# Row statistics of the feed-forward one step later, and two banks of attention products copied in one VectorE operation

## The reference, cut to what matters

```python
x = x + recurrence(layernorm(x))                 # tanh recurrence, 512 time steps, 8 sequences of 512 x 128
y = layernorm(x)
for i in range(6):                               # depth
    y = attn_layer(shift_tokens(y), Wqkv[i], q_scale[i], k_scale[i], Wo[i]) + y
    y = ffn_layer(shift_tokens(y), ln_g[i], ln_b[i], W1[i], b1[i], W2[i], b2[i]) + y
x = x + y

def attn_layer(x, ...):                          # 16 heads of 64, windows of 32 tokens
    q, k, v = split(x @ Wqkv)
    q, k = l2norm(q) * qs, l2norm(k) * ksc       # then rotary tables with cos, sin and a scale
    out = local_attention(q, k, v)               # each window of 32 queries sees its own and the window before
    return out @ Wo
def ffn_layer(x, g, bln, W1, b1, W2, b2):        # 128 -> 2 x 341 -> 128
    xn = (x - mean(x)) / sqrt(var(x) + 1e-5) * g + bln
    a, gate = split(xn @ W1 + b1)
    return a * gelu(gate) @ W2 + b2
```

## Time and profile before

| | before |
|---|---|
| time, median of 3 runs | 3390.91 us (3388.34 to 3396.97) |
| profiled execution, its own time | 3384.15 us |
| its span, first to last instruction | 3382.4 us |
| granted TensorE clock, mean | 0.993 of full speed |
| PE busy | 3262.9 us, 96% of the span |
| DVE busy | 2728.5 us, 81% |
| POOL busy | 2563.7 us, 76% |
| ACT busy | 2227.8 us, 66% |

### The profile page before, as it was taken

How to read it: one execution, slowest core, us unless ns; L and a number is a source line. 1 busy time by engine, 2 the same in 40 slices (tenths; PEclk the granted TensorE clock), 3 DMA queues, 4 the chain that set the end, 5 groups by cost and what they waited for, 6 DMA issues and landing times. The chain is left out here.

```text
span 3382.4 us, 101399 instructions
## 1 busy us (share of the span) xinstructions
PE 3262.9 (96%) x42193; PEld 2153.0 (64%) x42193; DVE 2728.5 (81%) x3698; ACT 2227.8 (66%) x4397; POOL 2563.7 (76%) x2957
## 2 busy tenths in 40 slices
PE   8999699999999999999999999999999999999996
PEld 5555366666666666666666666666666666666664
DVE  2333598888988888888888888888888888888883
ACT  2222367767777777776776777777767777777674
POOL 0000498888888888888888888888888888888882
PEclk9999899999999999999999999999999999999999
DMA  3000001000001000001000010000010000000000
GB/s 74 1 1 1 4 11 36 12 11 8 12 17 36 8 11 11 11 15 36 11 12 8 11 42 12 10 9 11 11 43 8 12 11 11 12 13 18 14 9 13
DMA packets 62284, 52.53 MB, mean 16 GB/s; under 512 B 11526, under 2 KB 59396, under 8 KB 61828
## 3 DMA queue, kind: packets, MB, share of 16 engines
q1 hardware_dynamic: 61828, 46.05, 5.2%
HBM read 43.93 MB, written 2.10 MB: 14 GB/s over the span
## 5 line engine op out<-in xcount | busy, mean ns | idle before, releaser
L477 POOL TENSOR_TENSOR cosp<-cosp,sinp 128x1024 f32<-128x1024 f32 x384 | 905.6, 2373 | 26.5 <-DVE sinp L976 24.3
L584 PE MATMUL ps<-w_qk,xs 128*128 128x512 f32 x1536 | 747.8, 609 | 11.6 <-ACT sq L792 7.9
L688 PEld LDWEIGHTS ps<-px,w_vo 128*128 128x128 f32 x6144 | 701.0, 192 | 54.2 <-ACT px L833 38.8
L467 POOL TENSOR_TENSOR cosp<-cosp,rr 128x1024 f32<-128x1024 f32 x384 | 723.1, 1904 | 11.4
L688 PE MATMUL ps<-px,w_vo 128*128 128x128 f32 x6144 | 721.8, 276 | 3.7 <-ACT px L833 1.7
L973 DVE TENSOR_TENSOR cosp<-ps,tab 128x1024 f32<-128x1024 f32 x384 | 469.9, 1224 | 253.5 <-PE ps L584 250.2
L792 ACT ACTIVATE sq<-ps 128x1024 f32<-128x1024 f32 x384 | 393.4, 1024 | 338.1 <-DVE sinp L976 338.1
L584 PEld LDWEIGHTS ps<-w_qk,xs 128*128 128x128 f32 x1536 | 262.9, 191 | 342.9 <-issue 342.9
L976 DVE TENSOR_TENSOR sinp<-ps,tab 128x1024 f32<-128x1024 f32 x384 | 466.5, 1215 | 0.0
L737 PE MATMUL ps<-pT,xtm 32*128 32x512 f32 x3072 | 435.5, 615 | 24.4 <-DVE pT L1050 13.4
L982 DVE TENSOR_REDUCE ss<-sq 128x16 f32<-128x1024 f32 x384 | 454.5, 1184 | 3.1 <-POOL rr L452 1.8
(11 more groups left out here) (110 smaller groups left out, 4760.8 us busy)
## 6 DMA issues: line engine op xcount, KB each, us to landing
tab<-in_tab SPq DMA_DIRECT2D x96, 128.0 KB, 2.1
qks<-in_scales SPq DMA_DIRECT2D x96, 128.0 KB, 3.5
w_qk<-in_L_ffn_Wqkv SPq DMA_DIRECT2D x12, 512.0 KB, 6.4
w_v<-in_wv_t SPq DMA_DIRECT2D x6, 512.0 KB, 8.0
w_o<-in_L_ffn_Wo SPq DMA_DIRECT2D x6, 512.0 KB, 8.4
x<-in_L_attn_x SPq DMA_DIRECT2D x16, 128.0 KB, 6.0
out<-w_v SPq DMA_DIRECT2D x16, 128.0 KB, 2.5
w<-in_L_ffn_W SPq DMA_DIRECT2D x6, 341.0 KB
```

The costliest lines, as they stand in the source:

```text
L467: eng.tensor_tensor(v, v, rr[:, B % 2, HEADS * i:HEADS * i + HEADS].unsqueeze(2).to_broadcast([P, HEADS, DH]), ALU.mult).then_inc(rot_read ...
L477: eng.tensor_tensor(cosp[:, A % 2, i, :], cosp[:, A % 2, i, :], sinp[:, i, :], ALU.add).then_inc(rot_added, 1)
L584: t = eng.matmul(ps[:, u, :], xs[:, n % ROUND, :], w_qk[:, n // TILES % 2, i, 512 * u:512 * u + 512], start=True, stop=True)
L688: t = eng.matmul(Y, w_vo[:, E // TILES % 2, i // HP, i % HP, :], px[:, i, :], start=i == 0, stop=i == HEADS - 1)
```

## The change

It does two things. The statistics of a turn move from lag 7 to lag 8: on VectorE from behind the gated product to a place between the residual sum of E and the rotary multiplications of the keys; with them the four extra columns of the inverse root (ScalarE and GpSimd) move from step 4T+7 to 4T+8, `shift` to 4T+9, and ScalarE's normalisation to step 4T+9, between its copies to `qT` and its copies to `kT`. And ScalarE copies two banks of products instead of three, while VectorE copies banks 1 and 2 in one operation of 128x1024. TensorE's order stays the same; two of its waits count differently.

```diff
-        normed = lambda s: min(s, NT) * REFINE
-        rooted = lambda s: min(s, NT) * 2
+        rounds_before = lambda s: min(s, NT) + (s > NT) + (s > NT + ROUND)
+        normed = lambda s: rounds_before(s) * REFINE
+        rooted = lambda s: rounds_before(s) * 2
...
@@ GpSimd step
-                T = turn_of(s, 8)
+                T = turn_of(s, 9)
                 if T is not None:
-                    eng.wait_ge(norm_step, normed(s) if s <= NT else normed(s) + REFINE)
+                    eng.wait_ge(norm_step, normed(s))
                     after(eng, xn_ready, TB * T)
                     eng.wait_ge(variance_done, 2 * T + 2)
-                    eng.tensor_tensor(shift[:, :], nmean[:, :], rr[:, 1, 2 * HEADS:], ALU.mult).then_inc(shift_done, 1)
+                    eng.tensor_tensor(shift[:, :], nmean[:, :], rr[:, 0, 2 * HEADS:], ALU.mult).then_inc(shift_done, 1)
...
-                T = turn_of(s, 7)
+                T = turn_of(s, 8)
                 if T is not None:
                     eng.wait_ge(stat_step, 2 * TB * T + 2 * TB)
...
@@ TensorE step
-                    after(eng, px_evac, 3 * E + 2)
+                    after(eng, px_evac, 2 * E + 2)
                     eng.transpose(X, xs[:, C % ROUND, :], ident[:, :]).then_inc(xt_done, 1)
                 if tile(E):
-                    eng.wait_ge(px_evac, 3 * (E + 1))
+                    eng.wait_ge(px_evac, 2 * (E + 1))
                     eng.wait_ge(px_last, E + 1)
...
@@ ScalarE
+            def normalised(T):
+                eng.wait_ge(shift_done, T + 1)
+                eng.wait_ge(rows_evac, T + 1)
+                after(eng, cols_done, T)
+                for i in range(TB):
+                    at = 2 * HEADS + i
+                    eng.activation(xn[:, i, :], xr[:, i, :], ACT.Identity, bias=shift[:, i:i + 1], scale=rr[:, 0, at:at + 1]).then_inc(xn_ready, 1)
...
-                    for i, b in enumerate((3, 0, 1)):
+                    for i, b in enumerate((3, 0)):
                         eng.wait_ge(px_done, 4 * E + i + 1)
...
+                    if turn_of(s, 9) is not None:
+                        normalised(turn_of(s, 9))
                     if turn_of(s, 10) is not None:
                         eng.activation(warm[:, 1:2], warm[:, 0:1], ACT.Gelu)
                     for u, k in enumerate(K_BANKS):
...
@@ VectorE step
+                T8 = turn_of(s, 8)
+                if T8 is not None:
+                    statistics(T8)
                 if tile(A):
                     rope(A, 1)
...
-                T7, T13 = turn_of(s, 7), turn_of(s, 13)
-                if T7 is not None:
-                    statistics(T7)
+                T13 = turn_of(s, 13)
                 if T13 is not None:
                     update(T13)
...
-                    eng.tensor_copy(px[:, :, 64:96], G(2).rearrange("p (h q) -> p h q", q=WIN)).then_inc(px_last, 1)
+                    eng.tensor_copy(px[:, :, 32:96].rearrange("p h (b q) -> p b h q", q=WIN),
+                                    ps[:, 5:7, :].rearrange("p b (h q) -> p b h q", q=WIN)).then_inc(px_last, 1)
```

More of the change, by code:

```diff
@@ L794, in ffn @@
             def ffn(s):
[L795 to L802, removed]
                 T = turn_of(s, 9)
@@ L873, in step @@
                         eng.copy(dst, G(k).rearrange("p (h b t) -> p h b t", h=4, b=GB)).then_inc(turn_evac, 1)
+                T = turn_of(s, 9)
+                if T is not None and not tile(B):
+                    normalised(T)
                 T = turn_of(s, 7)
```

## The result

The changed kernel takes 3406.11 us (median of 6 runs, 3404.15 to 3411.69), the kernel before beside it 3389.28: ratio 1.005, 95% interval 1.0037 to 1.0062. It is slower by 0.5%, where "no change" was the forecast and 3392 the number; it lies 0.9 us inside the upper end of the range, 3407. The profiled execution took 3411.69 us, the longest of its six, with a span of 3409.9 us.

What follows compares the result with a forecast made beforehand. TensorE was taken as held in step mod 0 by GpSimd, late behind VectorE's statistics. Terms -29 (mod 0), +27 (mod 1), +8 (mod 2), -5 (results) sum to +1: 3385 profiled, 3392 as median, range 3372 to 3407.

Steps and rivals of the forecast that it cites:

- no change: Whole kernel: measured time within 0.3% (about 10 us) of the kernel before, chance 0.60.
- step mod 0: Steps with s mod 4 = 0: statistics no longer delay GpSimd's chain and the query turning; 16.07 becomes 15.23 us, gain 0.84.
- the query rotary starts at 2.47: VectorE, every step: behind the longer copy the query rotary starts at 2.47 us instead of 2.02, 0.45 later.
- the new wait for the normalisation: Steps mod 1: TensorE's `xn` transposes wait 0.58 us for ScalarE's normalisations, in 46 rounds: +27 us.
- VectorE did not become the bound: Rival, every step: no idle time left on VectorE, so the longer copy costs 102 us, 3493; chance 0.03.
- the steps with a result: Last five rounds: the result's sum no longer stands behind the statistics on VectorE; 1.05 us forward each, -5 us.
- 6.37 + 0.65 + 8.68 = 15.70: Steps mod 0 in the 20 rounds with fused weights: key projection, fusing, rest of step; 16.33 becomes 15.70, gain 0.63.
- The gelus: Steps mod 2: ScalarE's last two gelus end about 0.40 later, next step starts 0.24 later; 35 rounds, +8 us.
- The holes: TensorE inside the scores: 19 holes of about 0.9 us, about 11 in steps mod 2 covering the gelu delay.
- 46 rounds that have all parts: Basis of the sum: per-step gains and losses over 46 pipeline rounds, plus the last rounds, together +1 us.
- The same 0.45: ScalarE behind the query rotary: the squares of the queries and all behind move 0.45 us; squares hidden by 0.5.
- a dearer copy: Rival: VectorE's two-bank copy costs more than 1.22 us; at 1.37 it gives +21, 3413; chance 0.12.

Runs made afterwards that it cites:

- Run 3: Changed kernel with ScalarE's four normalisations moved right behind the exponential in step 4T+9: 3376.15 us, ratio 0.9963 to the kernel before.
- run 7: Changed kernel with 32 unused transposes (64 TensorE instructions) added at its start, shifting the instruction blocks: 3409.02 us, ratio 1.0061 to the kernel before.
- run 8: Kernel before with the same 32 unused transposes (64 TensorE instructions) added at its start: 3389.94 us, ratio 1.0009 to the kernel before.
- Run 2: Kernel before with only the copies changed (ScalarE two banks, VectorE two in one operation), statistics and normalisation unmoved: 3399.92 us, ratio 1.0031.
- run 5: Kernel of run 3 with ScalarE's copies `xc` also moved behind the exponential in steps mod 3: 3366.04 us, ratio 0.9933 to the kernel before.
- run 9: Kernel before with an extra ScalarE scratch copy of 0.42 us ahead of the copies to qT in steps mod 3: 3389.66 us, ratio 1.0003.
- run 10: Kernel before with the same extra ScalarE copy, but between the copies to qT and those to kT, in steps mod 3: 3394.13 us, ratio 1.0016.
- run 1: Changed kernel with the copies put back (ScalarE three banks, VectorE one), so only the statistics and normalisation move: 3367.60 us, ratio 0.9938 to the kernel before.
- run 4: Kernel of run 1 with ScalarE's normalisations moved behind the exponential in step 4T+9: 3359.43 us, ratio 0.9915 to the kernel before.

## Why the prediction was right and where it failed

**Right.** The step mod 0 was held by the statistics: the key projection is back at 6.37 and the step gains 0.86 (forecast 0.84). The copy costs 1.220, the query rotary starts at 2.47, the new wait for the normalisation is there in 46 rounds and costs 0.62 (0.58). Run 3, which takes that wait away, confirms its price. VectorE did not become the bound: the step mod 3 is still 14.40, and 0.80 of idle time is left in the step mod 1. In the last rounds the steps with a result went from 16.15 to 15.11, the 1.05 of the forecast. In the usual steps the sum is +1.8 for tiles 12 to 167, against a forecast of +1 for the pipeline.

**Mis-sized.** "6.37 + 0.65 + 8.68 = 15.70" for fused rounds: with the fusing in front, the output starts 0.74 later than in a round without it (2097.87 - 2095.20 = 2.67 against 2036.44 - 2034.51 = 1.93) and takes 0.1 longer, and the step is 15.90. That is 20 x 0.2 = 4 us. The gelus, "+0.24" a step, cost 0.07: in 35 rounds 2.5 us instead of 8. The two errors about cancel. The holes were also miscounted: "about 11 fall in steps mod 2", where the trace before shows 8 of 0.48 us or more.

**Failed.** The sum was taken over "46 rounds that have all parts" as if a round always took its usual time, and the holes inside the scores entered it only as a cover ("TensorE has holes of about 0.9 inside the scores, 19 in all"). They were taken as a constant. They are late fetches of instructions; in steps mod 3 these start 0.4 us later with the change, some of them 1.4 to 1.8 later, the waits grew from 17.9 to 30.6 us, and behind the longest ones TensorE ran at 1.2 GHz. In the profiled pair this is 23 of 27.5 us, in the pair of runs 7 and 8 it is 12 of 23. The text named it as what would make it wrong ("if the holes inside the scores multiply"), and gave it no chance and no price. The same 0.45 had been followed through "all that ScalarE does behind" and judged hidden wherever an operation of TensorE did not wait; a fetch does not show as such a wait. Run 2 places the larger part of the growth with the copy, in steps mod 3 nearly all of it. Runs 5, 9 and 10 show that the end of the copies to qT and kT moves the fetches and the gaps; only runs 5 and 10 show it in the time too.

**Luck.** That 3406 lies inside the range at all is luck. The range reached up to 3407 to cover a dearer copy, and the copy cost what the forecast said. "Slower by over 0.3%", which is what came, had a chance of 0.18 on record, and nothing of it was for the holes.

**Open.** Why a fetch follows the copies to qT in one case and those to kT in another: in steps 59 and 91 it changed from the earlier group to the later one, in step 179 and in step 79 of run 10 the other way, at the same instruction. In step 59 it changed even in run 1, where no copy in that step is later. And how the loss of 16.8 us between the medians is divided: the usual steps and short rounds give 5, so 12 are left for gaps and clock, as many as in the pair of runs 7 and 8, and of those runs 9 and 10 account for 1 to 5 by the steps mod 3. The rest lies in the gaps of the other steps and of the fused ones, and was not separated. The part of the clock is uncertain as well: the profiled execution of the changed kernel had a mean clock of 0.989, its other five 0.991 to 0.993, so the rows show more of the lower level than the medians hold.

## What to carry to other kernels

Sum the usual rounds of a pipeline, but look apart at what its unusual ones wait for: a wait that has no releaser and recurs at a fixed count of instructions points to the supply of instructions. Here its length went with the end of ScalarE's copies, which no operation of TensorE had to wait for. A slower operation that is hidden on every engine can come back that way. And when two edits are bundled, price each with the other in place: here the statistics' move alone is worth 22 us (30 with the normalisation in ScalarE's idle time), and the copy costs 11 us alone and 39 beside it.

## What the hardware showed that I had not expected

TensorE's instructions arrive in blocks of 16 KB, and the scores, 256 instructions in 1.5 us, outrun the fetch, which in steps mod 3 starts 2.3 to 2.7 us before TensorE resumes. And a gap of two microseconds in an otherwise full pipeline can be followed by a stretch at 1.2 GHz: five of six gaps from 2.0 us up had one behind them in the changed kernel, so that a wait of 2.4 us in step 59 cost 3.75. It is no sharp line: of gaps near 1.9 us those of run 4 (1.86 and 1.92) had one behind them, and the 1.92 of the kernel before had none, nor had one of 2.37 in step 79 of run 2.
